# Graph network kernel: three GpSimd sums moved behind the last gather of attention, eight tiles gathered beside the queries, unread query rows dropped

## Chip, cores and metric

One core of a Trainium2 chip. The time is device microseconds of one launch; lower is better.

## The reference, cut to what matters

Four graph layers follow one another on 3125 nodes of 64 features and 103125 edges (sorted by target): a propagation of 10 hops, three graph convolutions, an edge attention with two heads, and a message layer. The change lies in the attention layer:

```
q = (h @ Wq + bq).reshape(n, HEADS, C)
k = (h @ Wk + bk).reshape(n, HEADS, C)
v = (h @ Wv + bv).reshape(n, HEADS, C)
e = (edge_attr @ We).reshape(-1, HEADS, C)
qi = q[tgt];  kj = k[src] + e;  vj = v[src] + e
alpha = jnp.sum(qi * kj, axis=-1) / math.sqrt(C)
a = softmax of alpha over the edges of one target
agg = segment_sum(a[:, :, None] * vj, tgt)
out = agg.reshape(n, HC) @ Wp + bp + h
out = out + gelu(layernorm(out) @ W1 + b1) @ W2 + b2
```

## The kernel before, in words

The kernel is a row of stages, each a block in which every engine has its own program; a stage ends when all engines are through, and then the next begins. Three stages matter here.

**stage_attend_tables** (L1356) makes what attention needs. SyncE writes the normed node rows `hn` to the DRAM table `row_table` (x_t, L1382), loads biases and weights (L1384 to L1391), and writes the queries to `q_table` group by group (L1396, seven groups), with the keys for a later stage between them (L1399). TensorE turns `hn` (L1435), multiplies (L1442, L1452); ScalarE copies (L1464, L1470) and VectorE scales and copies (L1498, L1508), and shifts keys (L1490, L1502). ScalarE waits at L1458 for GpSimd's second memset. GpSimd sets the pair weights and 32 unread rows of the query tile to zero (L1405, L1407), makes a column of numbers (L1409), reduces the largest |hn| over the partitions (L1412, after VectorE's L1491) and then adds bias rows to `h` and `xs` and `h` to `xs` (L1415, L1417, L1419), which stage_nodes reads.

**stage_attend** (L1511) walks over tiles of 256 edges: T1 = 403 tiles, and V2 = 451 visits of a tile to one block of 64 targets. Tile t needs its source rows, two indirect gathers of 128 rows by GpSimd (L1594), unless it is one of those that TensorE picks out of a table in SBUF: `picked` gives 48 tiles, the last two of each 16 from tile 16 on, so FETCHED holds 355 tiles and GpSimd issues 710 gathers. Their slots are a ring of R = 8:

```
for n, t in enumerate(FETCHED):
    if n >= R:
        po.wait_ge(turned, step_of_tile(FETCHED[n - R]))
```

A step i of TensorE turns tile i + 2 (L1620, when both gathers and the edge load have landed), turns the weights of visit i - 3 (L1625), computes masks and scores of visit i (L1634, L1637), does its share of the picks (L1645) and sums visit i - 5 (L1655). VectorE makes one-hot masks (L1712), takes the maximum (L1739) and small differences (L1745, L1750, L1759) and adds into `acc` (L1756). ScalarE exponentiates. Before the first step VectorE sets `acc` to zero (L1703), and at step 3 it runs `split` (L1720 to L1729), which makes the table for the picks. The last 48 visits have no new tile.

**stage_nodes** (L1768) starts when attention is through.

Of the kernel before, what the change touches and what calls it, by code (L numbers as in the profile page):

```python
# [10 lines left out]
I32 = mybir.dt.int32  # L11
# [6 lines left out]
P = 128  # L18
NODES = 3125
EDGES = 103125  # L20
D = 64
# [80 lines left out]
def along(v, k):  # L102

    return v.unsqueeze(1).to_broadcast([P, k, v.shape[1]])


class Mem:


    def __init__(self, nc, ctx):  # L110
# [15 lines left out]
        self.iotaH = sb("iotaH", [P, CW], F16)  # L126
        self.colsN = sb("colsN", [P, 8, NCH], F32)
        self.smalls = self.work2[:, 3 * DC + NCH * D:3 * DC + NCH * D + 8 * D]
        self.PS = ctx.enter_context(nc.psum_tensor("banks", [P, 8, 512], F32))
# [61 lines left out]
def stage_tables(nc, m, last0, last, dst, src, edges):  # L191
# [4 lines left out]
    with ExitStack() as ctx:  # L196
# [58 lines left out]
        def _(po):  # L255
            po.iota(iotaI, pattern=[[1, V0P]], base=0, channel_multiplier=0).then_inc(s_iota, 1)
            for s in schemes:
                po.iota(s["tI"], pattern=[[P, s["C"]]], base=0, channel_multiplier=1).then_inc(s_iota, 1)
            po.memset(m.ident[:, :], 0.0).then_inc(s_pool, 1)
            po.wait_ge(s_pool, 1)  # L260
# [1080 lines left out]
def step_of_tile(t):  # L1341

    return t + 1
# [11 lines left out]

def stage_attend_tables(nc, m, keep, s_in, x_out, q_out, w_in, w1, w2, w3, bp, bb2, b3, g2, b2, b1, x_t, q_t, src, keys_t):  # L1356

    with ExitStack() as ctx:
        sem = lambda n: ctx.enter_context(nc.semaphore(n))
        take = Take(m.big)  # L1360
        take.at = keep["end"]
        late = keep["end"] + JPAD + P + RT * 2 * XW + RT * TE - JN * P
# [4 lines left out]
        w_out = keep["w_out"]  # L1367
        hn, xs, h = m.node(2), m.node(0), m.node(3)
        pair_w, rows, cols = keep["pair_w"], keep["rows"], keep["cols"]
# [6 lines left out]
        nodes_in = lambda g: len(chunks(g)) * P  # L1376
        gm, gall, downI = m.colsN[:, 7, 0:1], m.colsN[:, 7, 1:2], m.colsN[:, 7, 8:9].bitcast(I32)
        block = ctx.enter_context(nc.Block())

        @block.sync  # L1380
        def _(sp):
# [10 lines left out]
            for g in range(NG):  # L1392
                sp.wait_ge(x_taken0, g + 1)
                sp.wait_ge(x_taken1, g + 1)
                j = slice(2 * GROUP * g, 2 * GROUP * g + 2 * len(chunks(g)))
                sp.dma_start(q_t[j, :, :].rearrange("j p n -> p j n"), q_all[:, j, :]).then_inc(q_out, 16)  # L1396
                if g == NG - 3:
                    sp.wait_ge(s_keys, SHIFTS)
                    sp.dma_start(keys_t.rearrange("k (p f) -> p k f", p=P), shifted).then_inc(m.first_landed[1], 16)  # L1399
            sp.wait_ge(m.first_landed[1], 32)  # L1400
            sp.wait_ge(w_in, WEIGHTS_IN)

        @block.gpsimd
        def _(po):
            po.memset(pair_w, 0.0).then_inc(s_zero, 1)  # L1405
            po.wait_ge(s_zero, 1)
            po.memset(q_all[D + DE:P, :, :], 0.0).then_inc(s_zero, 1)  # L1407
            po.wait_ge(s_zero, 2)
            po.iota(downI, pattern=[[0, 1]], base=-CENTER, channel_multiplier=-1).then_inc(s_zero, 1)  # L1409
            po.wait_ge(s_zero, 3)  # L1410
            po.wait_ge(m.max_in, 6)
            po.partition_all_reduce(gall, gm, P, bass.bass_isa.ReduceOp.max).then_inc(m.max_out, 1)  # L1412
            po.wait_ge(m.max_out, 6)
            po.wait_ge(w_in, WEIGHTS_IN)
            po.tensor_tensor(h, h, along(rows[:, 0:D], NCH), ALU.add).then_inc(s_zero, 1)  # L1415
            po.wait_ge(s_zero, 4)
            po.tensor_tensor(xs, xs, along(rows[:, D:2 * D], NCH), ALU.add).then_inc(s_zero, 1)  # L1417
            po.wait_ge(s_zero, 5)
            po.tensor_tensor(xs, xs, h, ALU.add)  # L1419

# [35 lines left out]
        def _(act):  # L1456
            act.dma_start(srcI, src.rearrange("(p f) -> p f", p=P)).then_inc(m.first_landed[0], 16)
            act.wait_ge(s_zero, 2)  # L1458

# [19 lines left out]
        def _(dve):  # L1479
# [8 lines left out]
            ins.then_inc(s_wo, 1)  # L1488
            dve.wait_ge(m.first_landed[0], 32)
            dve.tensor_scalar(shifted[:, 0, :], srcI, float(-CENTER), None, ALU.add).then_inc(s_keys, 1)  # L1490
            dve.tensor_reduce(gm, hn.rearrange("p a d -> p (a d)"), op=ALU.max, axis=X, apply_absolute_value=True).then_inc(m.max_in, 1)  # L1491
            dve.wait_ge(s_zero, 2)
            for g in range(NG + 1):
                if g < NG:
                    n = nodes_in(g)
                    dve.wait_ge(q_done, g + 1)
                    wait(dve, x_done, g - 1)
                    dve.tensor_scalar(qf[g % 2][:, 0:n], m.PB[2 + g % 2][:, 0:n], bq_c, float(D) ** -0.5, ALU.add, ALU.mult).then_inc(q_ready, 1)  # L1498
                if 1 <= g < SHIFTS:
                    if g == 1:  # L1500
                        dve.wait_ge(s_keys, 1)
                    dve.tensor_scalar(shifted[:, g, :], shifted[:, 0, :], float(-P * g), None, ALU.add).then_inc(s_keys, 1)  # L1502
                if g >= 1:
                    b = g - 1
                    n = nodes_in(b)
                    dve.wait_ge(x_done, b + 1)
                    j = slice(2 * GROUP * b, 2 * GROUP * b + n // BD)
                    dve.tensor_copy(q_all[0:XW, j, BD:P], m.PB[6 + b % 2][0:XW, 0:n].rearrange("p (j d) -> p j d", d=BD)).then_inc(x_taken1, 1)  # L1508


def stage_attend(nc, m, keep, x_out, q_out, ea, ea_t, src, x_t, q_t):  # L1511
# [4 lines left out]
    with ExitStack() as ctx:  # L1516
# [6 lines left out]
        iota2 = take(P // 2).bitcast(F16)  # L1523
        rows = take(RT * 2 * XW).rearrange("p (t s c) -> p t s c", t=RT, s=2)
        XF = take(RT * TE).rearrange("p (t e) -> p t e", t=RT)
# [18 lines left out]
        hot = [more(TE).bitcast(F16) for _ in range(AHOT)]  # L1544
        hn = m.node(2)
        table = m.node(1).rearrange("p a d -> p (a d)").bitcast(F16).rearrange("p (a s d) -> p a s d", a=NCH, s=2)
        gall, downI = m.colsN[:, 7, 1:2], m.colsN[:, 7, 8:9].bitcast(I32)

        init = sem("av_init")
        turned = sem("av_turned")  # L1550
        copied = sem("av_copied")
# [12 lines left out]
        def _(sp):  # L1564
            own = Walk(nc, m, "block", mybir.EngineType.SP)
            for v in range(V2):
                if v < T1:
                    wait(sp, turned, step_of_tile(v - R))
                    wait(sp, summed, v - RT + J2)
                    tile = ea[v:v + 1, :, :].rearrange("t p n -> p (t n)").rearrange("p (s c) -> p s c", s=2)  # L1570
                    sp.dma_start(rows[:, v % RT, :, D:D + DE], tile).then_inc(m.landed_e[v % R], 16)
                    if picked(v):
# [9 lines left out]
                if v == 0:  # L1582
                    sp.wait_ge(q_out, 16 * NG)
                sp.dma_start(qT[v % R], q_t[bass.ds(j, 1), :, :].rearrange("j p n -> p (j n)")).then_inc(m.landed_q[v % R], 16)

        @block.gpsimd
        def _(po):
            po.wait_ge(x_out, 16)
            for n, t in enumerate(FETCHED):
                if n >= R:  # L1590
                    po.wait_ge(turned, step_of_tile(FETCHED[n - R]))
                wait(po, summed, t - RT + J2)
                for s in range(2):
                    po.indirect_dma_start(rows[:, t % RT, s, 0:D], None, x_t.rearrange("a p c -> (a p) c"), bass.IndirectOffsetOnAxis(  # L1594
                        ap=m.src2[:, s, t:t + 1], axis=0)).then_inc(m.landed_g[n % R], 16)

        @block.tensor
        def _(pe):
            pe.wait_ge(init, 1)
            own = Walk(nc, m, "slot", mybir.EngineType.PE)  # L1600
            for i in range(-TURN_AHEAD, V2 + SUM_BEHIND):
                t, u = i + TURN_AHEAD, i - P_BEHIND
                if u < V2:
# [93 lines left out]
        def _(dve):  # L1697
# [3 lines left out]
            for hd in range(HEADS):  # L1701
                dve.tensor_copy(iota2[:, hd * BD:(hd + 1) * BD], m.iotaH[:, 0:BD])
            dve.memset(acc, 0.0).then_inc(init, 1)  # L1703
            dve.wait_ge(init, 1)
            chain = m.dve_step.on(dve)
            own = Walk(nc, m, "block", mybir.EngineType.DVE)
# [9 lines left out]
            def split():  # L1716

                dve.wait_ge(q_out, 16 * NG)
                for t in range(AG - 2, RT, AG):
                    dve.memset(XF[ONE:ONE + 1, t:t + 2, :], 1.0)  # L1720
                dve.tensor_copy(down, downI)
                dve.tensor_copy(comb[0:D, :], m.ident[0:D, 0:D])
                dve.tensor_copy(comb[D:P, :], m.ident[D:P, D:P])
                chain(dve.tensor_scalar(wexp, gall.bitcast(I32), 0x7F800000, None, ALU.bitwise_and))
                chain(dve.tensor_scalar(wexp, wexp, float(87 << 23), None, ALU.max))
# [581 lines left out]
def build(nc, last0, last, x, src, dst, edges, ea, ea_t, ef, L0_gnn_W, L0_gnn_b, L1_gnn_W1, L1_gnn_b1, L1_gnn_W2, L1_gnn_b2, L1_gnn_W3,  # L2307
# [4 lines left out]
    with ExitStack() as ctx:  # L2312
# [26 lines left out]
        stage_attend_tables(nc, m, keep, at_in, x_out, q_out, w_in, L2_gnn_W1, L2_gnn_W2, L3_gnn_W1[D:, :], L2_gnn_bp, L2_gnn_b2, L3_gnn_b1,  # L2339
                            L2_gnn_ln2_g, L2_gnn_ln2_b, L2_gnn_b1, x_t, q_t, src, keys_t)  # L2340
        stage_attend(nc, m, keep, x_out, q_out, ea, ea_t, src, x_t, q_t)
# [42 lines left out]
```

## Time and profile before

| | us |
|---|---|
| runs (median of 3) | 3213.01 |
| lowest and highest run | 3197.84, 3217.87 |
| span of the profiled execution | 3198.0 |
| stage_attend_tables, first and last work | 1350.9 to 1389.3 |
| stage_attend, first gather to the next stage's first product | 1390.3 to 2356.4 |

The span runs from the first to the last instruction of one execution. The profile gives no time of that execution beside its span; the lowest of the three runs is 0.2 us off the span, the median 15.0 us above it. Times are read as microseconds from the span's start.

### The profile page before, as it was taken

To read this page: it belongs to the slowest core of one execution; us is meant where nothing else is said; L and a number is where in the kernel's file an instruction comes from. 1 tells how busy PE (TensorE), PEld (TensorE's weight loads), DVE (VectorE), ACT (ScalarE), POOL (GpSimd) and SP (SyncE) were. 2 spreads that over 40 slices of the span, in tenths; PEclk is the share of its full clock that TensorE was granted. 3 is DMA by queue.
4 is the path that set the end of the run, shared out by engine and by line. 5 is a ranking of instruction groups with operands and counts; after the bars stand their busy time and mean duration, and the time that the engine had idled before them with its cause. 6 is when DMAs were issued, how large, how long until landed. Compare 5 with 4: busy or idle time off the path is not lost. (4 is left out here: it accounts for less than half of the span.)

```text
span 3198.0 us, 70441 instructions
## 1 busy us (share of the span) xinstructions
PE 2723.7 (85%) x18621; PEld 1834.2 (57%) x18621; DVE 2250.6 (70%) x6702; ACT 1612.0 (50%) x4685; POOL 1512.6 (47%) x1604
## 2 busy tenths in 40 slices
PE   2777777799998499759888888998986999999998
PEld 1566665355554244337777777776874555555556
DVE  6999998566665312657777777777887777777772
ACT  1788887033332000035555555555664666666666
POOL 2121122044443000067777777777405777777770
PEclk6999999899999799869999999999997999999995
DMA  1122222056557755543333333333203555445540
GB/s 38 73 91 89 91 89 89 21 195 204 196 197 257 270 238 238 223 102 80 84 81 81 82 85 79 83 83 82 63 21 98 127 131 131 127 128 130 131 112 12
DMA packets 446966, 378.15 MB, mean 118 GB/s; under 512 B 174376, under 2 KB 385416, under 8 KB 446632
## 3 DMA queue, kind: packets, MB, share of 16 engines
q1 hardware_dynamic: 396184, 315.64, 32.3%
q0 software_dynamic: 40896, 43.60, 6.7%
q10 hardware_dynamic: 9552, 14.75, 1.3%
q8 instruction: 175, 2.87, 0.4%
q14 instruction: 159, 1.30, 0.1%
HBM read 286.75 MB, written 87.03 MB: 117 GB/s over the span
## 5 line engine op out<-in xcount | busy, mean ns | idle before, releaser
L1594 POOL DMA_INDIRECT big<-row_table,src x710 | 675.0, 951 | 217.1 <-issue 171.6
L2080 POOL DMA_INDIRECT big<-message_table,src x542 | 532.6, 983 | 228.2 <-issue 154.2
L2119 PE MATMUL banks<-big 128*128 128x512 f16 x1650 | 422.6, 380 | 8.9 <-DVE big L2194 8.9
L2212 DVE TENSOR_SCALAR big<-big 128x2048 f16<-128x2048 f16 (+2 forms) x396 | 422.4, 1067 | 1.3 <-DMA big<-shifted_keys 0.7
L507 PE MATMUL banks<-work 128*128 128x226 f16 x1197 | 312.3, 261 | 104.2 <-ACT banks L538 41.4
L899 PE MATMUL banks<-big,work 128*128 128x512 f16 (+1 forms) x1750 | 350.0, 359 | 17.0 <-DVE work L1041 17.0
L964 POOL TENSOR_TENSOR work<-work 128x400 f16<-128x400 f32 x196 | 180.2, 945 | 280.5 <-DVE work L1033 220.3
L1739 DVE TENSOR_REDUCE big<-banks 128x1 f32<-128x256 f32 x451 | 190.2, 422 | 173.1 <-PE banks L1637 159.7
L1637 PE MATMUL banks<-big 97*128 x902 | 303.4, 419 | 0.7
L508 PE MATMUL banks<-work 128*128 128x200 f16 x1197 | 300.5, 251 | 0.0
L509 PE MATMUL banks<-work 128*128 128x200 f16 x1197 | 298.6, 249 | 0.0
L450 POOL COPY work<-work 128x100 f16<-128x100 f16 x120 | 86.2, 723 | 380.9 <-DVE work L473 361.8
L1680 ACT ACTIVATE big<-big 128x1 f32<-128x1 f32 x451 | 91.6, 203 | 346.5 <-DVE big L1750 336.2
L899 PEld LDWEIGHTS banks<-big,work 128*128 128x128 f16 x1750 | 157.9, 101 | 188.2 <-DVE work L1041 17.3
L2156 ACT ACTIVATE big<-iotaH,rel 128x64 f32<-128x64 f16 x902 | 258.5, 334 | 5.5 <-DVE big L2171 3.9
L2128 PEld LDWEIGHTS banks<-big 128*64 128x64 f32 x1804 | 148.4, 145 | 184.9 <-issue 183.9
L1115 PE MATMUL banks<-big,work 128*128 128x512 f16 x900 | 202.7, 386 | 55.8 <-DVE work L1199 52.0
L1620 PE MATMUL banks<-ident,big 128*97 128x128 f32 x710 | 145.9, 288 | 100.0 <-issue 68.2
L928 ACT CAST work<-work 128x400 f16<-128x400 f32 x196 | 100.8, 525 | 238.8 <-DMA work<-weights_dense 238.0
L2128 PE MATMUL banks<-big 128*64 x1804 | 212.5, 244 | 7.8 <-issue 2.8
L2119 PEld LDWEIGHTS banks<-big 128*128 128x128 f16 x1650 | 153.4, 98 | 114.2 <-DVE big L2194 9.2
L533 ACT ACTIVATE work<-banks 128x800 f32<-128x800 f32 x196 | 163.5, 834 | 97.7 <-PE banks L509 89.9
(373 smaller groups left out, 6143.4 us busy)
## 6 DMA issues: line engine op xcount, KB each, us to landing
big<-weights_halves SPq DMA_DIRECT2D x10, 6400.0 KB, 24.0
big<-shifted_keys SPq DMA_DIRECT2D x66, 640.0 KB
weights_dense<-work SPq DMA_DIRECT2D x196, 200.0 KB, 1.9
work<-weights_dense SPq DMA_DIRECT2D x196, 200.0 KB, 2.7
weights_halves<-work SPq DMA_DIRECT2D x98, 400.0 KB, 2.9
big<-q_table SPq DMA_DIRECT2D x451, 64.0 KB
big<-in_ef SPq DMA_DIRECT2D x403, 64.0 KB
big<-in_ea SPq DMA_DIRECT2D x403, 32.0 KB
```

Source lines behind the costliest of these rows:

```text
L507: pe.matmul(to(CW, CW + CAW), rows[:, 0, t, :], cols[:, t, :], start=False, stop=True, skip_group_check=True)
L508: pe.matmul(to(0, CW), rows[:, 1, t, :], cols[:, t, 0:CW], start=False, stop=True, skip_group_check=True)
L509: pe.matmul(to(0, CW), rows[:, 2, t, :], cols[:, t, 0:CW], start=False, stop=True, skip_group_check=True).then_inc(vis_done, 1)
L899: ins = pe.matmul(m.PB[c % 4][:, 0:width(c)], z[k][:, a, :, :], m.counts(c)[:, a, :], start=(a == 0), stop=(a == NCH - 1))
L1115: pe.matmul(out, z[l % 2][:, a, :, :], weights[:, :, s, a * BP:(a + 1) * BP], start=(a == 0 and s == 0), stop=False)
L1594: po.indirect_dma_start(rows[:, t % RT, s, 0:D], None, x_t.rearrange("a p c -> (a p) c"), bass.IndirectOffsetOnAxis(ap=m.src2[:, s, t:t + ...
L1637: pe.matmul(psS[v % 3], qT[v % R][0:XW, :], XF[0:XW, bass.ds(slot, 1), :].rearrange("p t e -> p (t e)"), start=False, stop=True).then_inc( ...
L2080: po.indirect_dma_start(G[n % R][:, s, :], None, g_t.rearrange("a p c -> (a p) c"), bass.IndirectOffsetOnAxis(ap=m.src2[:, s, t:t + 1], ax ...
L2119: pe.matmul(psH[q % 2], table[:, a, :, :].rearrange("p s d -> p (s d)"), hot[:, 2 * TE * a:2 * TE * (a + 1)], start=(a == 0), stop=(a == N ...
L2128: ins = pe.matmul(psA[v % 3], oh[v % 4][:, s, :], M[:, bass.ds(slot, 1), s, :].rearrange("p t c -> p (t c)"), start=(s == 0), stop=(s == 1))
L2156: ins = nc.scalar.activation(away[v % 2][:, s, :], m.iotaH[:, 0:BD], ACT.Abs, bias=m.rel2[:, s, v:v + 1], scale=-1.0)
L2212: dve.tensor_scalar(hot[:, 2 * TE * a:2 * TE * (a + n)], key[q % 2][:, 0:n, :], place[:, BATCHES.index((a, n)):BATCHES.index((a, n)) + 1], ...
```

## The change

Six edits. In stage_attend_tables GpSimd loses the memset of the unread rows, the column of numbers (made once in stage_tables, `m.below`), the reduction over partitions and the three sums; it zeroes `acc` and then gathers the first eight tiles once `row_table` has landed. SyncE loads the edge features of those eight tiles behind the queries. ScalarE's wait for GpSimd goes, and VectorE takes the maximum of `hn` behind its last query copy in place of ahead of the first. Only 97 of the 128 rows of each query tile are written and read back. In stage_attend GpSimd starts with the ninth fetched tile and does the three sums after its last gather; VectorE writes a single row of ones where it zeroed `acc`, and the maximum over partitions is taken by a TensorE transpose, a VectorE reduction of one row and a TensorE product that spreads it.

```diff
         self.colsN = sb("colsN", [P, 8, NCH], F32)
+        self.below = self.colsN[:, 7, 8:9].bitcast(I32)
...
                 po.iota(s["tI"], pattern=[[P, s["C"]]], base=0, channel_multiplier=1).then_inc(s_iota, 1)
+            po.iota(m.below, pattern=[[0, 1]], base=-CENTER, channel_multiplier=-1)
...
-def stage_attend_tables(nc, m, keep, s_in, x_out, q_out, w_in, w1, w2, w3, bp, bb2, b3, g2, b2, b1, x_t, q_t, src, keys_t):
+def attend_rows(m, keep):
+
+    at = keep["end"] + JPAD + P
+    return m.big[:, at:at + RT * 2 * XW].rearrange("p (t s c) -> p t s c", t=RT, s=2)
+
+
+def fetch(po, m, rows, x_t, n):
+
+    t = FETCHED[n]
+    for s in range(2):
+        po.indirect_dma_start(rows[:, t % RT, s, 0:D], None, x_t.rearrange("a p c -> (a p) c"), bass.IndirectOffsetOnAxis(
+            ap=m.src2[:, s, t:t + 1], axis=0)).then_inc(m.landed_g[n % R], 16)
+
+
+def load_edges(sp, m, rows, ea, t):
+
+    tile = ea[t:t + 1, :, :].rearrange("t p n -> p (t n)").rearrange("p (s c) -> p s c", s=2)
+    sp.dma_start(rows[:, t % RT, :, D:D + DE], tile).then_inc(m.landed_e[t % R], 16)
...
+        edge_rows = attend_rows(m, keep)
         take = Take(m.big)
-        take.at = keep["end"]
+        take.at = keep["end"] + JPAD + P + R * 2 * XW
...
-                sp.dma_start(q_t[j, :, :].rearrange("j p n -> p j n"), q_all[:, j, :]).then_inc(q_out, 16)
+                sp.dma_start(q_t[j, 0:XW, :].rearrange("j p n -> p j n"), q_all[0:XW, j, :]).then_inc(q_out, 16)
                 if g == NG - 3:
                     sp.wait_ge(s_keys, SHIFTS)
                     sp.dma_start(keys_t.rearrange("k (p f) -> p k f", p=P), shifted).then_inc(m.first_landed[1], 16)
+            for t in range(R):
+                load_edges(sp, m, edge_rows, ea, t)
             sp.wait_ge(m.first_landed[1], 32)
             sp.wait_ge(w_in, WEIGHTS_IN)
...
         @block.gpsimd
         def _(po):
             po.memset(pair_w, 0.0).then_inc(s_zero, 1)
-            po.wait_ge(s_zero, 1)
-            po.memset(q_all[D + DE:P, :, :], 0.0).then_inc(s_zero, 1)
-            po.wait_ge(s_zero, 2)
-            po.iota(downI, pattern=[[0, 1]], base=-CENTER, channel_multiplier=-1).then_inc(s_zero, 1)
-            po.wait_ge(s_zero, 3)
-            po.wait_ge(m.max_in, 6)
-            po.partition_all_reduce(gall, gm, P, bass.bass_isa.ReduceOp.max).then_inc(m.max_out, 1)
-            po.wait_ge(m.max_out, 6)
-            po.wait_ge(w_in, WEIGHTS_IN)
-            po.tensor_tensor(h, h, along(rows[:, 0:D], NCH), ALU.add).then_inc(s_zero, 1)
-            po.wait_ge(s_zero, 4)
-            po.tensor_tensor(xs, xs, along(rows[:, D:2 * D], NCH), ALU.add).then_inc(s_zero, 1)
-            po.wait_ge(s_zero, 5)
-            po.tensor_tensor(xs, xs, h, ALU.add)
+            po.memset(keep["acc"], 0.0)
+            po.wait_ge(x_out, 16)
+            for n in range(R):
+                fetch(po, m, edge_rows, x_t, n)
...
             act.dma_start(srcI, src.rearrange("(p f) -> p f", p=P)).then_inc(m.first_landed[0], 16)
-            act.wait_ge(s_zero, 2)
...
             ins.then_inc(s_wo, 1)
-            dve.wait_ge(m.first_landed[0], 32)
-            dve.tensor_scalar(shifted[:, 0, :], srcI, float(-CENTER), None, ALU.add).then_inc(s_keys, 1)
-            dve.tensor_reduce(gm, hn.rearrange("p a d -> p (a d)"), op=ALU.max, axis=X, apply_absolute_value=True).then_inc(m.max_in, 1)
-            dve.wait_ge(s_zero, 2)
...
                     dve.tensor_scalar(qf[g % 2][:, 0:n], m.PB[2 + g % 2][:, 0:n], bq_c, float(D) ** -0.5, ALU.add, ALU.mult).then_inc(q_ready, 1)
+                if g == 0:
+                    dve.wait_ge(m.first_landed[0], 32)
+                    dve.tensor_scalar(shifted[:, 0, :], srcI, float(-CENTER), None, ALU.add).then_inc(s_keys, 1)
...
                     dve.wait_ge(x_done, b + 1)
                     j = slice(2 * GROUP * b, 2 * GROUP * b + n // BD)
                     dve.tensor_copy(q_all[0:XW, j, BD:P], m.PB[6 + b % 2][0:XW, 0:n].rearrange("p (j d) -> p j d", d=BD)).then_inc(x_taken1, 1)
+            dve.tensor_reduce(gm, hn.rearrange("p a d -> p (a d)"), op=ALU.max, axis=X, apply_absolute_value=True)
...
-        rows = take(RT * 2 * XW).rearrange("p (t s c) -> p t s c", t=RT, s=2)
+        rows = attend_rows(m, keep)
+        take(RT * 2 * XW)
...
+        gtop, one_row = m.colsN[0:1, 7, 9:10], more(P, 1)
 
         init = sem("av_init")
+        s_top, tops = m.max_in, 5
...
                 if v < T1:
                     wait(sp, turned, step_of_tile(v - R))
                     wait(sp, summed, v - RT + J2)
-                    tile = ea[v:v + 1, :, :].rearrange("t p n -> p (t n)").rearrange("p (s c) -> p s c", s=2)
-                    sp.dma_start(rows[:, v % RT, :, D:D + DE], tile).then_inc(m.landed_e[v % R], 16)
+                    if v >= R:
+                        load_edges(sp, m, rows, ea, v)
...
                 wait(sp, scored, v - R + 1)
                 if v == 0:
                     sp.wait_ge(q_out, 16 * NG)
-                sp.dma_start(qT[v % R], q_t[bass.ds(j, 1), :, :].rearrange("j p n -> p (j n)")).then_inc(m.landed_q[v % R], 16)
+                sp.dma_start(qT[v % R][0:XW, :], q_t[bass.ds(j, 1), 0:XW, :].rearrange("j p n -> p (j n)")).then_inc(m.landed_q[v % R], 16)
 
         @block.gpsimd
         def _(po):
-            po.wait_ge(x_out, 16)
-            for n, t in enumerate(FETCHED):
-                if n >= R:
-                    po.wait_ge(turned, step_of_tile(FETCHED[n - R]))
-                wait(po, summed, t - RT + J2)
-                for s in range(2):
-                    po.indirect_dma_start(rows[:, t % RT, s, 0:D], None, x_t.rearrange("a p c -> (a p) c"), bass.IndirectOffsetOnAxis(
-                        ap=m.src2[:, s, t:t + 1], axis=0)).then_inc(m.landed_g[n % R], 16)
+            for n in range(R, len(FETCHED)):
+                po.wait_ge(turned, step_of_tile(FETCHED[n - R]))
+                wait(po, summed, FETCHED[n] - RT + J2)
+                fetch(po, m, rows, x_t, n)
+            po.tensor_tensor(h, h, along(bias_rows[:, 0:D], NCH), ALU.add).then_inc(s_top, 1)
+            po.tensor_tensor(xs, xs, along(bias_rows[:, D:2 * D], NCH), ALU.add).then_inc(s_top, 1)
+            po.wait_ge(s_top, tops + 5)
+            po.tensor_tensor(xs, xs, h, ALU.add)
...
             pe.wait_ge(init, 1)
             own = Walk(nc, m, "slot", mybir.EngineType.PE)
+            pe.transpose(psH[0:1, 0:P], gm, m.ident[:, :]).then_inc(s_top, 1)
             for i in range(-TURN_AHEAD, V2 + SUM_BEHIND):
+                if i == 2:
+                    pe.wait_ge(s_top, tops + 2)
+                    pe.matmul(psH[:, TE:TE + 1], one_row, gtop, start=True, stop=True).then_inc(s_top, 1)
...
-            dve.memset(acc, 0.0).then_inc(init, 1)
+            dve.memset(one_row, 1.0).then_inc(init, 1)
             dve.wait_ge(init, 1)
+            dve.wait_ge(s_top, tops + 1)
+            dve.tensor_reduce(gtop, psH[0:1, 0:P], op=ALU.max, axis=X).then_inc(s_top, 1)
...
                 for t in range(AG - 2, RT, AG):
                     dve.memset(XF[ONE:ONE + 1, t:t + 2, :], 1.0)
-                dve.tensor_copy(down, downI)
...
+                dve.wait_ge(s_top, tops + 3)
+                chain(dve.tensor_copy(gall, psH[:, TE:TE + 1]))
                 chain(dve.tensor_scalar(wexp, gall.bitcast(I32), 0x7F800000, None, ALU.bitwise_and))
```

## Rows read from the trace of the kernel before

**Rows 1.** The page's busy time, and its row of the gathers.

```profile
PE 2723.7 (85%) x18621; PEld 1834.2 (57%) x18621; DVE 2250.6 (70%) x6702; ACT 1612.0 (50%) x4685; POOL 1512.6 (47%) x1604
...
L1594 POOL DMA_INDIRECT big<-row_table,src x710 | 675.0, 951 | 217.1 <-issue 171.6 <-PE banks L1655 29.0 <-PE banks L1625 15.5
```

**Rows 2.** Timeline of GpSimd (POOL): start, duration, operation, idle before it.

```profile
1351.38 5.43 POOL L1407 MEMSET big<- 32x6400 f32 x1
...
1370.72 0.38 POOL L1412 PARTITION_ALL_REDUCE colsN<-colsN  x1 [5.95 <-issue]
1378.52 3.54 POOL L1415 TENSOR_TENSOR work<-work 128x1600 f32<-128x1600 f32 x1 [7.43 <-issue]
...
1385.77 3.55 POOL L1419 TENSOR_TENSOR work<-work 128x1600 f32<-128x1600 f32 x1
1390.29 1.19 POOL L1594 DMA_INDIRECT big<-row_table,src  x1 [0.97 <-POOLq L1358]
```

**Rows 3.** The same view later: ninth tile's first gather, a slow gather, the last.

```profile
1410.54 0.94 POOL L1594 DMA_INDIRECT big<-row_table,src  x1 [0.30 <-issue]
1414.28 1.87 POOL L1594 DMA_INDIRECT big<-row_table,src  x1 [0.30 <-issue]
2280.48 0.95 POOL L1594 DMA_INDIRECT big<-row_table,src  x1 [0.30 <-issue]
```

**Rows 4.** Waits of TensorE in 1420 to 2270: total, times, longest.

```profile
PE banks L1620 <- issue: 65.4, 65, 2.6
```

**Rows 5.** Timeline of the queries (TensorE, ScalarE, VectorE, SyncE), and a later edge load.

```profile
1352.79 1.91 PE L1435 MATMUL banks<-ident,work 128*64 128x128 f32 x8
1355.96 1.28 DVE L1490 TENSOR_SCALAR big<-big 128x806 f16<-128x806 int32 x1 [2.67 <-DMA big<-in_src]
1356.83 1.06 ACT L1464 COPY big<-banks 64x512 f32<-64x512 f32 x2 [8.02 <-POOL big L1407]
1374.36 0.89 DVE L1508 COPY big<-banks 97x512 f32<-97x512 f32 x2
1375.14 2.80 SPq L1396 DMA_DIRECT2D q_table<-big  x2
1391.89 0.57 SPq L1571 DMA_DIRECT2D big<-in_ea  x1
```

**Rows 6.** The source view of the row table's write: time to landing.

```profile
DMA to landing us min/median/max: 6.7/6.7/6.7
```

**Rows 7.** Timeline of attention's start.

```profile
1389.81 0.17 DVE L1698 MEMSET big<- 128x128 f32 x1 [14.55 <-PEq L1358]
1391.49 5.23 DVE L1703 MEMSET big<- 128x6208 f32 x1 [1.24 <-issue]
1396.78 1.17 PE L1620 MATMUL banks<-ident,big 128*97 128x128 f32 x4 [22.03 <-DVE big L1703]
1401.78 0.94 POOL L1594 DMA_INDIRECT big<-row_table,src  x1 [0.30 <-issue]
1404.41 0.71 PE L1620 MATMUL banks<-ident,big 128*97 128x128 f32 x2 [0.68 <-ACT big L1672]
```

**Rows 8.** The same view at the split, and a step at the full clock.

```profile
1408.13 2.11 DVE L1720 MEMSET big<- 1x512 f32 x4 [0.16 <-issue]
1413.45 1.88 DVE L1729 SCALAR_TENSOR_TENSOR work<-work,scales 128x1600 f16<-128x1600 f32 x1
1417.39 0.74 PE L1620 MATMUL banks<-ident,big 128*97 128x128 f32 x2 [2.21 <-ACT big L1675]
1420.33 0.63 PE L1620 MATMUL banks<-ident,big 128*97 128x128 f32 x2
```

**Rows 9.** Busy time by stretch: PE, PEld, DVE, ACT, POOL, granted clock.

```profile
1400.00:1436.00 36.00, 28.26 (x144) 22.06 (x143) 25.88 (x113) 17.01 (x55) 27.46 (x29) 0.71 0.36 77
2290.00:2300.00 10.00, 10.00 (x82) 9.38 (x81) 9.59 (x55) 6.48 (x24) 0.00 (x0) 1.00 0.18 52
```

**Rows 10.** Source view of GpSimd's copy L450, beside VectorE's products.

```profile
L450 POOL COPY work<-work x120: 265/536/3587, 85.6 to 533.4; 128x100 f16<-128x100 f16 x120
```

More of the change, by code:

```diff
@@ L1353, in gathers_before, with stage_attend_tables @@
     return -(-(len(FETCHED) - n % R) // R) * 16
-def stage_attend_tables(nc, m, keep, s_in, x_out, q_out, w_in, w1, w2, w3, bp, bb2, b3, g2, b2, b1, x_t, q_t, src, keys_t):
+def attend_rows(m, keep):
[9 more added lines that the diff above has]
+    sp.dma_start(rows[:, t % RT, :, D:D + DE], tile).then_inc(m.landed_e[t % R], 16)
+def stage_attend_tables(nc, m, keep, s_in, x_out, q_out, w_in, w1, w2, w3, bp, bb2, b3, g2, b2, b1, x_t, q_t, src, keys_t, ea):
     with ExitStack() as ctx:
         sem = lambda n: ctx.enter_context(nc.semaphore(n))
+        edge_rows = attend_rows(m, keep)
         take = Take(m.big)
-        take.at = keep["end"]
+        take.at = keep["end"] + JPAD + P + R * 2 * XW
         late = keep["end"] + JPAD + P + RT * 2 * XW + RT * TE - JN * P
@@ L1367, in stage_attend_tables @@
         w_out = keep["w_out"]
-        hn, xs, h = m.node(2), m.node(0), m.node(3)
+        hn = m.node(2)
         pair_w, rows, cols = keep["pair_w"], keep["rows"], keep["cols"]
@@ L1376, in stage_attend_tables @@
         nodes_in = lambda g: len(chunks(g)) * P
-        gm, gall, downI = m.colsN[:, 7, 0:1], m.colsN[:, 7, 1:2], m.colsN[:, 7, 8:9].bitcast(I32)
+        gm = m.colsN[:, 7, 0:1]
         block = ctx.enter_context(nc.Block())
@@ L1544, in stage_attend @@
         hot = [more(TE).bitcast(F16) for _ in range(AHOT)]
-        hn = m.node(2)
+        hn, xs, h = m.node(2), m.node(0), m.node(3)
+        bias_rows = keep["rows"]
         table = m.node(1).rearrange("p a d -> p (a d)").bitcast(F16).rearrange("p (a s d) -> p a s d", a=NCH, s=2)
-        gall, downI = m.colsN[:, 7, 1:2], m.colsN[:, 7, 8:9].bitcast(I32)
+        gm, gall = m.colsN[:, 7, 0:1], m.colsN[:, 7, 1:2]
+        gtop, one_row = m.colsN[0:1, 7, 9:10], more(P, 1)
         init = sem("av_init")
+        s_top, tops = m.max_in, 5
         turned = sem("av_turned")
@@ L1720, in split @@
                     dve.memset(XF[ONE:ONE + 1, t:t + 2, :], 1.0)
-                dve.tensor_copy(down, downI)
+                dve.tensor_copy(down, m.below)
                 dve.tensor_copy(comb[0:D, :], m.ident[0:D, 0:D])
                 dve.tensor_copy(comb[D:P, :], m.ident[D:P, D:P])
+                dve.wait_ge(s_top, tops + 3)
+                chain(dve.tensor_copy(gall, psH[:, TE:TE + 1]))
                 chain(dve.tensor_scalar(wexp, gall.bitcast(I32), 0x7F800000, None, ALU.bitwise_and))
@@ L2339, in build @@
         stage_attend_tables(nc, m, keep, at_in, x_out, q_out, w_in, L2_gnn_W1, L2_gnn_W2, L3_gnn_W1[D:, :], L2_gnn_bp, L2_gnn_b2, L3_gnn_b1,
-                            L2_gnn_ln2_g, L2_gnn_ln2_b, L2_gnn_b1, x_t, q_t, src, keys_t)
+                            L2_gnn_ln2_g, L2_gnn_ln2_b, L2_gnn_b1, x_t, q_t, src, keys_t, ea)
         stage_attend(nc, m, keep, x_out, q_out, ea, ea_t, src, x_t, q_t)
```

## The prediction

> **What bounds the kernel now.** I read the page's groups first. The gathers of attention stand on top, and the number to see is not their busy time but busy and idle together: 675.0 + 217.1 = 892.1 us for 710 gathers, 1.256 us each [rows 1]. First gather to last, 1390.29 to 2281.43, are 891.1 us [rows 2, 3]: GpSimd issues without a pause for the whole of attention. The idle share is called "issue" or put down to a TensorE line, but always with the same 0.30 us, so it belongs to the instruction and is no wait. TensorE has the most busy time of the kernel [rows 1], yet in this stage it waits 65.4 us ahead of turning a tile, for something the profile shows as nothing [rows 4]. That is the landing of a gather: the fifth tile's second gather ends at 1402.72 and its turn begins at 1404.41 [rows 7]. So until 2281 attention goes at GpSimd's pace of 2.51 us per fetched tile, and what counts is **when that chain starts and whether anything makes it stop**. After it come some 48 visits without a new tile, where TensorE is busy 10.00 of 10 us and VectorE 9.59, with 82 products, ten a step: 1.22 us a step [rows 9]. There the two engines bind together and GpSimd does nothing.
>
> Ahead of the chain, the timeline shows why it starts late. The query work is over at 1375.25 and SyncE's last issue at 1377.94 [rows 5]; GpSimd is in its reduction over partitions (5.95 us idle ahead, 7.43 behind, so a small result costs 13.7) and then in three sums, until 1389.32 [rows 2]. All engines wait for that.
>
> **Stage_attend_tables.** GpSimd's work becomes: the small memset until 1351.3, the memset of `acc` (6208 elements a row at the pace of 6400 in 5.43 us: 5.3) until 1356.7, the wait for the row table (issued at 1350.9, landed after 6.7 [rows 6]) until 1357.6, and 16 gathers of 1.256 us, 20.1, until 1377.7. The queries themselves start sooner: ScalarE's first copy stood until 1356.83 behind the memset that goes, though four of the eight turns that begin at 1352.79 are done by 1353.8 [rows 5]. That moves every group 3.0 us forward; the key shift of 1.28 us [rows 5] now falls behind the first scaling, into VectorE's wait for the second group, and costs nothing (if that cover were gone, 1.3). SyncE ends its queries at 1374.9 in place of 1377.9, and then issues eight edge loads. An edge load took 0.57 [rows 5], with 0.05 between: 5.0, so SyncE ends at **1379.9** and is the last. The unread rows save 31 of 128 rows in seven writes and 451 reads; the reads are hidden behind the gathers, so I take nothing for them, and up to 1 us in SyncE's queue, whose last two issues took 2.80 together [rows 5]. The stage ends 1389.3 - 1379.9 = 9.4 us sooner. By GpSimd alone it would be 11.6, the other end.
>
> **Start of attention.** From the stage's end to TensorE's first turn passed 1396.78 - 1389.32 = 7.5 us, of which 5.23 are the memset of `acc` [rows 7]. It goes, a row of ones comes (0.1). The first turn comes at 1382.1, and all eight tiles have landed. The ninth tile's first gather needs tile 0 turned, behind the turn of the maxima: some 0.8 us, 1382.9. Before, it was issued at 1410.54 [rows 3]. **The chain starts 27.6 us sooner**; of the 16 gathers that GpSimd no longer issues here (20.1 us) none stands on the path any more.
>
> **Does it stop after that?** It now has no spare slot, so each gather waits for a turn. TensorE is at the half clock there: 0.71 granted on average in the first 36 us [rows 9], the lower of its levels (1.2 GHz) until the step at 1417.39, which took 2.94 us to the next at 1420.33 [rows 8]. The split is the dangerous place: VectorE is away from 1408.13 to 1415.33 and tile 8 is turned 2.1 us later. Laid over the new start: steps of 2.2 to 2.9 us, split from about 1391.5 to 1398.8, tile 8 turned by 1401.5. GpSimd, 2.51 per tile from 1382.9, wants that slot at 1403.0, tile 9's at 1405.5 (turned 1404.4). It just fits; a miss costs 1 to 3 us, and I take 0. From there TensorE is faster (its 65.4 us of waiting are more than the lead of 8 x 2.51 = 20.1 us), so it uses up the lead and GpSimd binds as before. The maximum over partitions is now three tiny operations behind waits: VectorE's reduction has the first masks queued behind it, which TensorE needs for its first scores; about 0.5 us, not on GpSimd's chain. The wait in `split` for the spread maximum is over long before.
>
> **The three sums.** They move behind the last gather, 3.54 + 3.55 + 3.55 = 10.6 us [rows 2], where 48 steps of 1.22 us remain, so their own end is covered. But they read SBUF for 3.5 us at a stretch beside VectorE, which has 4% to spare there. No row shows VectorE beside such a sum; the nearest is GpSimd's small copy beside VectorE's two-input products, 265 ns at the least, 536 median, up to 3587 [rows 10]: one engine stands while the other has something. Price between 0 and 10.6 us. A step needs its small differences (two SBUF inputs each) before ScalarE can exponentiate, so I take near the full: 10.6 less about 2 us that TensorE has in hand, **8.5**. The Trainium skill, "SBUF — State Buffer", section "SBUF: two separate sides", says that GpSimd and a VectorE instruction with two SBUF inputs or in a 2-port mode take a shared port pair as an exclusive lock for the whole instruction; by that rule the price is near the upper end, and this change moves 10.6 us out of a place where VectorE was idle into one where it binds.
>
> **Sum.** 27.6 - 8.5 = 19.1 us off this execution's span: 3198.0 to 3178.9. The median of the runs lies 15.0 above that span, and I carry that over: 3213.0 - 19.1 = **3194**.
>
> **Rivals.**
> 1. *The sums cost nothing.* For it: the reductions of VectorE read one PSUM input, and 4% spare plus ScalarE's slack could take some. Against it: [rows 10]. Gain 27.6: 3185.
> 2. *The change doesn't do what it says in attention*: the eight tiles ahead bring nothing because TensorE's pace binds and GpSimd waits for turns. Then only TensorE's own start counts, 1396.78 - 1382.1 = 14.7, less 8.5: 6.2, 3207. Against it stand TensorE's 65.4 us of waiting [rows 4]; for it, only the cold first steps.
> 3. *The gathers are slow beside the queries.* One gather took 1.87 us while VectorE was in a long product [rows 3, 8]. If all 16 did, they would take 16 x 2.17 = 34.7, the stage would end at 1392.3 and the ninth tile start at 1395.3: 15.2 less 8.5 is 6.7, 3206. Against it: the other gathers of [rows 2, 7] ran at 0.94 beside a VectorE memset of 5.23. The Trainium skill's same section, in the box on DVE blocking DMA, has GpSimd unable to write descriptors while VectorE runs a 2-port operation. By that rule this is the outcome; the trace disagrees but for one gather.
> 4. *Slower*: TensorE stays at the lower clock. With no slot to spare, GpSimd would go at TensorE's 2.94 us a step: 16 steps are 47.0 us against 28 gathers in 35.1, 11.9 lost a round. The gain of 19.1 is gone after 26 such steps, and 48 of them give 3213 + 17 = 3230. It decides how long the clock stays low after the split; before, it rose at 1420 [rows 8], and busier engines argue against it.
>
> **How the numbers follow.** Forecast 0.52, rival 1 0.25, rival 2 0.10, rival 3 0.08, rival 4 0.05. The likeliest is 3194. The runs before lie 15 below to 5 above their median, and a new median may move by some 7 down and 5 up. Low end: rival 1 with GpSimd's end of the stage, 30 us, and the spread: 3176. High end: rivals 2 and 3 with the spread, 3212. A change of under 1% (32 us) can hardly be told from none by this kernel's runs, and 3181 is the bound of faster: a quarter to a third of rival 1, a little of the forecast and of what I have priced too low, 0.15. Slower by over 1% wants most of a hundred cold steps: 0.03.
>
> **What would show it.** Gathers from 1357.6 at 1.25 us each and the stage over near 1380; `acc` memset on GpSimd about 5.3 us; the ninth tile's gather near 1383, and no idle time over 0.3 us ahead of a gather, or little around the split; last gather near 2254; the sums behind it, with holes of some 3 us in VectorE and TensorE beside each and a tail of about 83 us (it was 75.0, 2281.4 to 2356.4). The prediction is wrong if GpSimd waits for turns over many rounds, if SyncE's edge loads are held up behind the query writes, or if the sums stretch the tail by nothing.

## The result, and the profile after

The changed kernel takes 3526.7 us (median; 3522.1 to 3537.0), against 3212.6 for the kernel before: a ratio of 1.099, 95% interval 1.095 to 1.102. It is slower by 314 us. The forecast was 3194 in a range of 3176 to 3212; neither it nor any rival comes near.

The table sets both executions on the start of stage_attend_tables (before 1350.9, after 1349.9), so that the stages ahead drop out. "Rest" is from stage_nodes' first product to the end of the span. The third column is the variant of the second experiment, shown here because two readings below lean on it.

| us behind the start of the tables stage | before | after | after, 128 rows |
|---|---|---|---|
| first turn of a tile | 45.9 | 136.5 | 34.4 |
| ninth tile's first gather | 59.6 | 137.4 | 35.3 |
| last gather over | 930.5 | 1190.8 | 908.4 |
| stage_nodes' first product | 1005.5 | 1326.9 | 994.5 |
| ninth tile's first gather to last gather (chain) | 870.9 | 1053.3 | 873.1 |
| last gather to stage_nodes (tail) | 75.0 | 136.2 | 86.1 |
| rest | 841.6 | 843.5 | 860.1 |

So the loss is in all three sections of attention, and in none of the stages before or behind. The timeline of the changed kernel's queues shows where it begins (start, duration, engine, operation, how many merged):

```profile
1357.31 1.19 POOL L1368 DMA_INDIRECT big<-row_table,src  x1 [1.81 <-DMA row_table<-work]
...
1376.27 0.95 POOL L1368 DMA_INDIRECT big<-row_table,src  x1 [0.30 <-issue]
```

```profile
1363.81 72.58 SPq L1419 DMA_DIRECT2D q_table<-big  x5
1436.44 18.11 SPq L1422 DMA_DIRECT2D shifted_keys<-big  x1
1454.64 21.04 SPq L1419 DMA_DIRECT2D q_table<-big  x2
```

GpSimd does what the prediction said: 16 gathers from 1357.3 at 1.25 us. But SyncE stands in its query writes. Five of them take 72.58 us of its queue, where two took 2.80 before [rows 5]; the key write behind them, 18.11. The edge loads stand behind them and begin at 1475.7, which the prediction had named as a sign of being wrong. The whole core waits for SyncE (busy time of each engine, then the granted clock, the mean busy share of the 16 DMA engines, and what they move):

```profile
core 0: us, PE busy (x) PEld busy (x) DVE busy (x) ACT busy (x) POOL busy (x), PEclk, DMA share, GB/s
...
1390.00:1438.00 48.00, 0.00 (x0) 0.00 (x0) 0.00 (x0) 0.00 (x0) 0.00 (x0) 0.50 0.07 22
```

For 48 us no engine works, and the DMA engines are busy to a share of 0.07, near one sixteenth. That number is the key to the case: the queue is full, and one engine of 16 empties it. The trace also records every DMA packet, though no view prints them one by one. From 1395 to 1430 it has 1488 packets of 512 bytes, one row each, in single file: each takes 27 ns and starts 23.5 ns after the one before (27 / 23.5 / 16 is the 0.07). The same in the source view of the write (duration in ns: least, median, most):

```profile
L1419 SPq DMA_DIRECT2D q_table<-big x7: 376/18142/19832, 1363.8 to 1455.8; - x7
```

In the walk over the tiles the gathers no longer bind. Here are the page's row of them, which answers to [rows 1], the waits of TensorE in 1500 to 2240, which answer to [rows 4], and the source view of the edge load:

```profile
L1368 POOL DMA_INDIRECT big<-row_table,src x710 | 677.4, 954 | 507.7 <-PE banks L1677 174.5
```

```profile
PE banks L1642 <- DMA big<-in_ea: 115.6, 179, 3.4
```

```profile
L1375 SPq DMA_DIRECT2D big<-in_ea x403: 606/1930/4426, 1475.7 to 2552.8; - x135
```

Before, the idle time ahead of gathers was 217.1 us of 0.30 each [rows 1]; now it is 507.7. Of the 291 us more, 110 are the ninth tile's first gather waiting for the late stage, and the others are waits for slots. TensorE's wait has a name now: the edge load, which the edit didn't touch. It stands in SyncE's queue behind the query read, and takes 1.93 us of that queue where the one in [rows 5] took 0.57. Between 1800 and 2100 there is no moment without a DMA packet, though the DMA share is 0.29; with 128 rows, at a share of 0.38, 44.5 us of 200 have none. Something is always busy, and it isn't the 16 engines together.

Behind the last gather the query reads stand alone, and the same pace shows bare (SyncE, TensorE, and the windows row of that stretch):

```profile
2598.58 40.91 SPq L1602 DMA_DIRECT2D big<-q_table  x18
```

```profile
2601.50 0.69 PE L1659 MATMUL banks<-big 97*128 x2 [0.88 <-DMA big<-q_table]
2603.76 0.69 PE L1659 MATMUL banks<-big 97*128 x2 [0.82 <-DMA big<-q_table]
```

```profile
2600.00:2680.00 80.00, 55.89 (x346) 46.58 (x345) 45.99 (x227) 27.80 (x99) 0.14 (x1) 0.91 0.07 20
```

18 reads in 40.91 us are 2.27 us each, and 97 rows of 23.5 ns are 2.28; TensorE waits for one in every step, which took 1.22 us before [rows 9]. The DMA share is 0.07 again.

### The profile page after: what moved, and what is told of

Its sections match the earlier page's. It is cut to its first block and busy times, and to the rows that moved or that the text cites. A ratio compares the mean times of both kernels' runs of the same rounds, so it can differ in the third digit from the quotient of the medians.

```text
span 3520.3 us, 70441 instructions
## 1 busy us (share of the span) xinstructions
PE 2813.8 (80%) x18624; PEld 1877.7 (53%) x18624; DVE 2260.0 (64%) x6704; ACT 1630.6 (46%) x4685; POOL 1538.0 (44%) x1603
## 5 line engine op out<-in xcount | busy, mean ns | idle before, releaser
L1368 POOL DMA_INDIRECT big<-row_table,src x710 | 677.4, 954 | 507.7 <-PE banks L1677 174.5
L1659 PE MATMUL banks<-big 97*128 x902 | 320.1, 439 | 33.0 <-DMA big<-q_table 32.9
L1642 PE MATMUL banks<-ident,big 128*97 128x128 f32 x710 | 155.4, 302 | 161.9 <-DMA big<-in_ea 158.6
L452 POOL COPY work<-work 128x100 f16<-128x100 f16 x120 | 108.7, 913 | 357.8 <-DVE work L475 338.7
L1694 ACT COPY big<-banks 97x256 f32<-97x256 f32 x355 | 130.7, 368 | 213.3 <-PE banks L1642 116.4
```

Source lines behind the costliest of these rows:

```text
L1659: pe.matmul(psS[v % 3], qT[v % R][0:XW, :], XF[0:XW, bass.ds(slot, 1), :].rearrange("p t e -> p (t e)"), start=False, stop=True).then_inc( ...
```

## The experiments

Every kernel was run beside the kernel before; ratios are to it, with their 95% intervals. The rest behind attention, which no experiment changes, takes between 841.6 and 866.7 us in the thirteen traces; so for steps of 10 us I go by the table's sections as well as by the medians.

**1. The row count alone.** The kernel before with

```diff
-sp.dma_start(q_t[j, :, :]..., q_all[:, j, :])
+sp.dma_start(q_t[j, 0:XW, :]..., q_all[0:XW, j, :])
-sp.dma_start(qT[v % R], q_t[bass.ds(j, 1), :, :]...)
+sp.dma_start(qT[v % R][0:XW, :], q_t[bass.ds(j, 1), 0:XW, :]...)
```

> The kernel before with one edit of the change alone: 97 of the 128 rows of each query tile are written and read back. Theory 1 (a transfer over 97 rows is spread over one or very few DMA engines, so each of the seven writes and each of the 451 reads takes many times longer): about as slow as the whole change, 3480 to 3560 us, with query writes of some 18 us each in SyncE's queue. Theory 2 (the loss comes from the eight tiles gathered early: no spare slot, GpSimd waits for turns): 3205 to 3215, as the kernel before.

Measured: 3521.1 us, ratio 1.100 (1.094 to 1.106). The sections are those of the whole change: first turn at 133.6, chain 1044.9, tail 135.1. The early tiles and the moved sums have no part in the loss that this run can tell from noise: stage_nodes starts at 1327.0, against 1326.9 with the whole change.

**2. Everything but the row count.** The changed kernel with `0:128` for `0:XW` at both places.

> The changed kernel with all 128 rows written and read; everything else of the change stays (the 31 rows beyond the 97 are not zeroed and nothing reads them). Theory 1: the forecast of the prediction, 3185 to 3194 us, the stage of the tables over near 1380 and the last gather near 2254. Theory 2: 3480 to 3530, with GpSimd's waits for TensorE as in the changed kernel.

Measured: 3203.2 us, ratio 0.999 (0.996 to 1.002). The 314 us are gone. The median lies 9 us above the forecast, though, and the comparison can't be told from no change. The table above shows most of why: at stage_nodes the gain is 11.0 us and not 19.1. Experiments 7 to 9 test its parts.

**3. One row more.** `0:98` at both places.

> The changed kernel with 98 rows instead of 97, written and read: one row more. Theory 1 by divisors (97 is prime and leaves one engine; the Trainium skill, DMA: Bandwidth & Descriptors, gives the largest number up to 16 that divides the row count, which is 14 for 98): within 10 us of the variant with 128 rows. Theory 1 in a form without divisors (any row count that is no multiple of 16 or 32 is slow): 3450 or more. Theory 2: 3480 to 3530.

Measured: 3204.0 us, ratio 0.998 (0.996 to 1.001); query writes of 490 ns median in SyncE's queue, chain 871.2. One row more of work gives 323 us back.

**4. 112 rows.**

> The changed kernel with 112 rows (7 x 16) written and read. Theory 1: all 16 engines are used, and as the reads are hidden behind the gathers it is within 3 us of the variant with 128 rows; a gain over it of more than 3 us would say that the bytes of the unread rows do cost something. Theory 2: 3480 to 3530.

Measured: 3203.2 us, ratio 0.999 (0.996 to 1.001), chain 872.5, stage_nodes at 994.3 against 994.5. The same as 128 rows: the bytes of the unread rows cost nothing that these runs can tell.

**5. Reads alone.** The changed kernel with writes of 128 rows and reads of 97.

> The changed kernel, with the query tiles written with 128 rows but read back with 97. If the few engines hurt writes and reads each for itself, the start of attention is as in the variant with 128 rows (first turn 34 to 36 us behind the start of the tables stage, not 136), and the walk stays slow: gathers over some 1050 us and a tail of some 136, in all about 3203 + 180 + 50 = 3433 us. If only the writes hurt and the walk was slow as a consequence of them: about 3205.

Measured: 3438.8 us, ratio 1.071 (1.064 to 1.078). First turn 34.4, chain 1058.9, tail 135.4. The two directions hurt separately: the reads cost 1058.9 - 873.1 = 186 us in the chain and 49 in the tail, the writes the other 102 us at the start (136.5 - 34.4).

**6. 106 rows, 2 x 53.**

> The changed kernel with 106 rows, 2 x 53, written and read. By divisors two engines carry each transfer: a query write takes about 18.1 x 106 / 97 / 2 = 9.9 us in SyncE's queue instead of 18.1, which moves the start of attention some 40 to 50 us back from the variant with 128 rows; a read is about halved too, to 1.3 us, and hidden behind the gathers; in all 3240 to 3260 us. If a row count just has to be even: 3203.

Measured: 3257.4 us, ratio 1.015 (1.008 to 1.021). First turn 85.9, chain 873.0. Source view and timeline of SyncE:

```profile
L1419 SPq DMA_DIRECT2D q_table<-big x7: 377/9867/11493, 1365.9 to 1416.6; - x7
```

```profile
1365.87 39.70 SPq L1419 DMA_DIRECT2D q_table<-big  x5
1405.62 9.89 SPq L1422 DMA_DIRECT2D shifted_keys<-big  x1
1415.60 12.46 SPq L1419 DMA_DIRECT2D q_table<-big  x2
```

The 9.9 us that were worked out came, and the first turn is 51.5 us later than with 128 rows where 40 to 50 were expected. An even count isn't enough. The counts measured are 97, 98, 106, 112 and 128: 97 is prime, 106 has 2 as its largest divisor up to 16, 98 has 14, the others 16. A write of eight tiles is 776 rows of 512 bytes in 18.14 us, 23.4 ns a row, or 848 in 9.87 over two, 23.3 ns a row on each. The reads of 106 rows are hidden again (by that pace 53 x 23.3 ns = 1.2 us each, an estimate); those of 97 (2.3 us, with the edge load in the same queue, and likely a share of it and of the gathers on the same engine) are not: a tile takes 1053.3 / 395 = 2.67 us where GpSimd needs 2.21 on the average over fetched and picked ones.

The Trainium skill, "DMA: Bandwidth & Descriptors", in the part on why a DMA increments its semaphore by 16, says that the number of engines is the largest up to 16 that divides the slowest dimension of both sides, and names 127 partitions as a case that ends on one. All five counts agree with it. The trace doesn't name the engine of a packet, but it shows how many rows are under way at once: one with 97 rows, and with 106 rows two, as from 1385 to 1400 in this run 1276 rows start 11.8 ns apart at 27 ns each. In the tail of experiment 3 a whole read of 98 rows is through in 0.3 to 0.6 us, where one of 97 takes 2.3. That 98 rows had just 14 engines is the page's number; here they are only seen to have many.

**7. Without the sums.** The variant with 128 rows, the four lines of sums behind the last gather deleted.

> The variant with 128 rows, without the three sums (the kernel leaves out the bias rows and the addition of h to the residual). If the sums hold VectorE for their whole length, the tail behind the last gather goes from 86 us back to 75, and the time from 3203 to 3192 us. If the longer tail has another cause (the clock, TensorE further behind at the last gather), it stays within 2 us of 86.

Measured: 3195.2 us, ratio 0.994 (0.992 to 0.997); tail 74.5. What the sums do is plain in the timeline of experiment 2, behind the last gather:

```profile
2260.58 3.55 POOL L1610 TENSOR_TENSOR work<-work 128x1600 f32<-128x1600 f32 x1 [7.03 <-issue]
...
2260.75 3.44 DVE L1736 TENSOR_SCALAR big<-big,rel 128x128 bf16<-128x128 f16 x1
...
2264.10 3.54 POOL L1611 TENSOR_TENSOR work<-work 128x1600 f32<-128x1600 f32 x1
2264.10 3.56 DVE L1771 TENSOR_TENSOR big<-big 128x1 f32<-128x1 f32 x1
...
2267.72 3.62 POOL L1613 TENSOR_TENSOR work<-work 128x1600 f32<-128x1600 f32 x1
...
2268.45 1.17 PE L1677 MATMUL banks<-big,work 128*128 x4 [5.87 <-DVE big L1782]
2268.51 2.88 DVE L1736 TENSOR_SCALAR work<-big,rel 128x128 bf16<-128x128 f16 x1
```

A VectorE mask of 0.25 us takes 3.44, and a subtraction of one column, normally 0.16, takes 3.56: each ends with the GpSimd sum beside it. Beside the third sum, VectorE's maximum from PSUM keeps its 0.41, and only then a mask is held, for 2.88. A one-column subtraction that began 0.03 us behind that sum's start was not held either; the trace doesn't say why. The three held instructions lost 3.19 + 3.40 + 2.63 = 9.2 us. The other 2 are likely the clock: TensorE stands 5.87 us, its granted clock is then at the lower level (0.50 from 2268.4 to 2276), and its products behind the pause run 1.17 where they ran 0.58. The windows of that stretch, with the sums and (experiment 8) without; the granted clock is 0.76 against 1.00:

```profile
2254.00:2282.00 28.00, 20.87 (x130) 18.64 (x131) 23.67 (x81) 10.08 (x37) 10.68 (x3) 0.76 0.10 29
```

```profile
2250.00:2282.00 32.00, 31.26 (x249) 29.11 (x248) 29.75 (x165) 20.54 (x75) 0.25 (x1) 1.00 0.18 50
```

**8. The sums on VectorE, in the tables stage.**

```diff
 dve.tensor_reduce(gm, hn..., op=ALU.max, axis=X, apply_absolute_value=True)
+dve.wait_ge(w_in, WEIGHTS_IN)
+dve.tensor_tensor(h, h, along(rows[:, 0:D], NCH), ALU.add)
+chain(dve.tensor_tensor(xs, xs, along(rows[:, D:2 * D], NCH), ALU.add))
+dve.tensor_tensor(xs, xs, h, ALU.add)
```

and the lines on GpSimd deleted; 128 rows.

> The variant with 128 rows, with the three sums on VectorE at the end of the tables stage, behind its maximum, three of 1.8 us where VectorE waits for SyncE and GpSimd anyway. The same theory: tail 75 us, the tables stage at most 1 us longer, 3192 to 3193 us, a ratio to the kernel before near 0.995. If the sums' place doesn't matter: 3203.

Measured: 3192.3 us, ratio 0.995 (0.992 to 0.997); tail 74.1, first turn 35.1. Three sums of 1.81 to 1.82 us in a place where VectorE then still waits 6.05. They are not free for GpSimd: two of its early gathers stand until a sum is over, 3.77 and 1.55 us for what takes 0.94:

```profile
1365.18 1.81 DVE L1526 TENSOR_TENSOR work<-work 128x1600 f32<-128x1600 f32 x1
1365.77 3.77 POOL L1368 DMA_INDIRECT big<-row_table,src  x1 [0.31 <-issue]
1366.91 1.82 DVE L1527 TENSOR_TENSOR work<-work 128x1600 f32<-128x1600 f32 x1
1368.76 1.82 DVE L1528 TENSOR_TENSOR work<-work 128x1600 f32<-128x1600 f32 x1
1369.85 1.55 POOL L1368 DMA_INDIRECT big<-row_table,src  x1 [0.30 <-issue]
1376.63 0.17 DVE L1722 MEMSET big<- 128x128 f32 x1 [6.05 <-PEq L1380]
```

The stage is not longer for it: the first turn of experiment 7, without any sums, is at 35.2.

**9. The early tiles undone.** The variant with 128 rows, `for n in range(len(FETCHED))` in stage_attend again and no gathers in the tables stage.

> The variant with 128 rows, but with the first eight tiles gathered at the start of attention again, as in the kernel before; the sums stay behind the last gather. If the eight early tiles are worth their 16 gathers, the last gather comes some 18 us later than in the variant with 128 rows (926 us behind the tables stage's start, not 908) and the time is near 3220 us, a little above the kernel before, since the longer tail is then hardly paid for. If they are worth nothing: 3203.

Measured: 3218.8 us, ratio 1.003 (1.001 to 1.005); last gather at 925.8, stage_nodes at 1012.0. Slower than the kernel before, for the sums now stretch the tail and nothing pays for it. The early tiles are worth 925.8 - 908.4 = 17.4 us.

**10. The sums in pieces.** 128 rows; each sum as 25 of 64 columns on GpSimd, at the same place.

> The variant with 128 rows, with each of the three sums cut into 25 pieces of 64 columns, still behind the last gather on GpSimd. If what costs is that VectorE stands until a GpSimd instruction has ended, short instructions cost it little: tail 76 to 80 us, 3193 to 3197 us. If it is the sums' total time or bytes on GpSimd: 86 us or more, as 75 instructions take longer than three.

Measured: 3195.9 us, ratio 0.996 (0.993 to 0.998); tail 80.8, a little over the expected 76 to 80. The pieces take 0.31 us each, 14 us for the first 50 alone, and cost about half of what three long sums do, though GpSimd is busy longer. So the cost doesn't go by GpSimd's busy time; it fits a VectorE that waits for one instruction's end.

**11. The early edge loads on ScalarE's queue.** Experiment 8 with `load_edges` moved behind ScalarE's last copy.

> The variant with the sums on VectorE, and with the eight early edge loads issued by ScalarE behind its last query copy instead of by SyncE behind the query writes. SyncE ends the tables stage now (7.0 us for the eight loads, 5.6 us behind GpSimd's last gather): without them the stage ends 4 to 5 us sooner and the time goes from 3192 to 3188 us. If the stage's end is set by something else: 3192.

Measured: 3190.2 us, ratio 0.994 (0.992 to 0.996); first turn 35.1, as in experiment 8. The expected 4 to 5 us did not come. ScalarE's queue now stands in the loads:

```profile
1368.39 9.16 ACTq L1375 DMA_DIRECT2D big<-in_ea  x7
```

What ends the stage can be read from its last instructions, in the source view of the line that closes it (DRAIN is over when the engine's work is; COMPARE_BRANCH is the last ahead of it on SyncE; EVENT_SEMAPHORE is where SyncE is let go):

```profile
L1380 POOLq DRAIN  x1: 20596/20596/20596, 1360.1 to 1360.1; - x1
L1380 SPq COMPARE_BRANCH  x1: 43/43/43, 1376.4 to 1376.4; - x1
L1380 ACTq DRAIN  x1: 402/402/402, 1377.6 to 1377.6; - x1
L1380 SPq EVENT_SEMAPHORE  x1: 17/17/17, 1380.9 to 1380.9; - x1
```

SyncE is through at 1376.6 and ScalarE at 1378.0, but GpSimd's drain ends at 1360.1 + 20.6 = 1380.7, and the stage with it. In experiment 8 the same view has GpSimd's drain over at 1376.2 and SyncE's at 1376.15, 33.9 and 33.8 us behind the stage's start. The expectation took SyncE for the last one there, but the two ended together, so taking the loads from SyncE alone could gain nothing. GpSimd is late because of the VectorE sums: its last early gather is over at 31.7 us and its drain at 33.9, against 28.1 and 32.5 in experiment 7, which has no sums.

## Why the prediction was wrong

**The step that failed** is "The unread rows save 31 of 128 rows in seven writes and 451 reads; the reads are hidden behind the gathers, so I take nothing for them". It counted bytes and took the engines that carry them as given. Measured instead, at stage_nodes: 97 rows cost 332 us against 128, of which the reads make 235 and the writes 97 (experiment 5; the writes cost 102 at the first turn, and the chain gives 5 back). All rows of a transfer went one behind the other at 23.5 ns each, so that a write held SyncE's queue for 18.1 us and a read took 2.3 us, too long to stay hidden behind GpSimd's 2.2 per tile. The prediction had a bound of 0 to 1 us of gain and none on the other side, and no rival. [rows 5] held only transfers of 128 rows, so no row gave the price of 97, and the text should have bounded it from the other side for just that reason. No view of the trace before would have told it; the rule in experiment 6, applied to 97, would.

**What bounds the kernel** was right: with 128 rows the chain is 873.1 us for 694 gathers, and shifting its start shifts its end (experiments 2 and 9: start at 35.3 and 54.1, last gather at 908.4 and 925.8).

**Start of the chain**: 27.6 us sooner forecast, 24.3 measured in experiment 2. SyncE ended the stage, as forecast. Three terms were off. SyncE does not profit from the earlier copies: it stands in the weight loads until 13.7 us behind the stage's start and ends its queries 25.7 behind it, against 27.0 before, 1.4 us gained and not 3.0. Eight edge loads took 7.00 us, not 5.0. And GpSimd was not through at its last gather, 27.1 us behind the stage's start, as the other end of the forecast (11.6 us for the stage) took it: its drain ended at 31.6, 1.5 ahead of SyncE's 33.1.

**No stop after it**: right. No gather beyond the ninth waited for a turn in experiment 2 (its idle time per gather stays 0.30). The chain is 2.2 us longer: the gather beside the split took 2.30 in place of 1.87, and the others make up the rest in small change, with a median of 947 ns in place of 944.

**The sums**: 8.5 forecast out of 0 to 10.6; measured 86.1 - 75.0 = 11.1, over the upper end, likely because the granted clock is at the lower level for some steps behind the pause. The mechanism was right, rival 1 wrong; the "2 us that TensorE has in hand" were not there. The durations in experiment 7 bear out the exclusive lock of the Trainium skill, "SBUF — State Buffer", section "SBUF: two separate sides"; they also show what it leaves free, a VectorE instruction whose only input is in PSUM, and the one-column subtraction beside the third sum, which has two SBUF inputs, doesn't fit.

**The sum without the rows**: 24.3 - 2.2 - 11.1 = 11.0 us, as stage_nodes shows (1005.5 to 994.5), against 19.1 forecast. In the medians it is 4.6 of 3207.8, inside the noise. Carrying the median 15 us above the span was sound for the size of the spread but gave no cause. Part of it is the rest behind attention, which varies by 25 us between traces; the execution profiled before had the shortest. In the eight variants within 1% of the kernel before, the medians gain 1 to 9 us less than the sections do, so the rest may be a little longer with the changed code; with one trace of the kernel before this stays open.

**Rival 2** named GpSimd waiting for turns, which the changed kernel shows, but with TensorE itself waiting for loads: not the mechanism. **Rival 3**: the 16 gathers beside the queries ran at 0.94 in experiment 2. What slows a gather is narrower than the rival had it: in the thirteen traces 17 gathers of attention took over 1.3 us, each beside a VectorE instruction with two SBUF inputs, 128x1600 (the split's product, and the sums of experiments 8 and 11). Each gather ended 0.81 to 0.82 us behind such an instruction, the longest two behind the second of two that followed on each other. Beside VectorE's maximum over 128x1600 (1.81 us) and the split's first product (1.88), which have one such input, none was slow. **Rival 4**: TensorE's products were at their full-clock length from 1402.6 in experiment 2 (0.39 for a pair of turns that took 0.63), 23 us behind its first turn.

## What to carry to other kernels

Before trimming a transfer, factor its row count: 98 rows went many at a time and 97 one at a time, and the row more was worth 323 us of 3527. If a stage ends in a queue that issues DMAs, read that queue's durations and the DMA share; here 0.07, with nothing else busy, meant one engine of 16. Work moved "behind" an engine is not free if it reads SBUF from GpSimd in long instructions while VectorE binds; on VectorE in an idle place it cost nothing here, though it held up two gathers by 3.4 us, which stayed hidden because SyncE ended the stage no sooner. 128 rows with the sums there is a version that beats both kernels (3192 us, ratio 0.995, interval 0.992 to 0.997).

## What the runs showed of the hardware that was not expected

- Rows of 512 bytes left 23.5 ns apart on what acted as one engine, at 27 ns a packet; with 106 rows the same pace showed twice over.
- Each of the 17 slow gathers of attention (1.55 to 3.80 us for what takes 0.94) was over 0.81 to 0.82 us behind the end of a VectorE instruction of 128x1600 with two SBUF inputs.
- The first sum after a run of gathers starts 7.03 us late, and in the kernel before 7.43 us behind the reduction [rows 2]; in experiment 10 6.98. It is put down to "issue". The prediction booked it as the reduction's cost. It comes behind gathers as well, so it isn't the reduction's alone. In all three traces a MODIFY_POOL_CONFIG instruction of GpSimd, which the timeline leaves out, stands 6.9 to 7.5 us ahead of the sum; the cause was not tried.
- A GpSimd sum and a VectorE mask or subtraction end together: 3.44 and 3.56 us for what takes 0.25 and 0.16.
